# A new order of VectorE, ScalarE and TensorE instructions from the last attention pair to the third expert, one split on GpSimd, and the last store in three pieces

## Chip, cores and metric

The kernel runs on one core of one Trainium2 chip. The metric is the device time of one execution in microseconds (us); lower is better. PE is TensorE, DVE is VectorE, ACT is ScalarE, POOL is GpSimd, and SP is the queue that issues the loads and stores.

## What is computed

One layer on 256 tokens of width 512, in float32, of three parts. The first is cross attention of the tokens to 4096 context rows and to themselves. The second is causal self attention with 16 heads and compressed queries and keys. The third, the one that fills the second half of the time, is a mixture of experts:

```python
scores = sigmoid(x @ router_w)                       # 32 experts in 8 groups
...                                                  # best 4 groups, best 8 experts in them
routed = sum over the chosen e of weight_e * (silu(x @ w_gate[e]) * (x @ w_up[e])) @ w_down[e]
shared = silu(x @ sw_gate) * (x @ sw_up) @ sw_down
return routed + shared
```

Each part works on a layer-normed input and adds its result to the residual.

## The kernel before

All 32 experts are computed for all 256 tokens and weighted, with weight 0 for those not chosen. The shared expert is cut in two and stands in front, so there are `NE` = 34 experts, numbered from 0.

**Split products.** Each float32 matrix product is made of three products of rounded parts (`product`, L410, L413, L414): a_hi b_hi, a_lo b_hi and a_hi b_lo. For every weight tile that comes from memory, ACT therefore rounds `raw` to `w_hi` (`split_hi`, L278) and DVE computes `w_lo` = `raw` - `w_hi` (`split_lo`, L283). For a result that goes into a later product, ACT reads the bank to the high part (L306 and L326, `out_hi`, `half_hi`) and DVE the low part (L310 and L331, `out_lo`, `half_lo`). The values of attention, the normed tokens and the hidden rows of each expert all pass this way: PE to ACT to DVE to PE.

**Tiles.** Weight tiles are numbered through the whole program and lie in two slots in turn. An expert's tile (896 + 640 KB) has three parts: k = 0 (128x1280: gate, and the first quarter of up), k = 1 (128x1024: down) and k = 2 (128x768: the rest of up). SP loads part 0 with one transfer, and parts 1 and 2 with another (part b). Each transfer waits until the low part of the tile that had the slot has been made (`load`, L362). All loads stand in one queue.

**Order.** There is no scheduler. Each engine has one list of instructions, written out by hand or in a loop, and runs it strictly in order; engines wait for one another on counting semaphores. An instruction that waits therefore holds all that stand behind it on its engine.

**The stretch around the change** (229 to 282 us of the trace):
- The last attention pair, for the first half h = 0 and the second half h = 1 of the tokens. PE makes scores (`score_last`), DVE masks them and takes the row maximum (`last_bias`, L1331, L1396), ACT takes exponentials (`last_exps`, L1053), DVE divides by their sum (`last_normalize`, L1402, L1407), PE transposes (`transpose_last`, L773), ACT and DVE split (`last_probs_hi`, `last_probs_lo`), PE multiplies with the values (`values_last`), ACT and DVE split again, and PE makes the output product (`out_pair`) with part 1 of the attention tile. The output product of the pair before, tile 27, is mixed in.
- The third layer norm (`add_to_residual` L1143, `norm_stats` L1128 to L1132, the root on POOL L1566, `normalize` L1138) and transposes of the tokens.
- Experts 0 and 1 in another form (`expert_rows`): the hidden rows come out by token, are multiplied (`rows_hidden`, L1441) and transposed (`transpose_hidden`, L826).
- The router: PE's scores (L882), ACT's sigmoid (L1089), and on DVE a chain of some 30 small dependent instructions (L1489 to L1531) that ends in `weights`.
- From expert 2 on a loop. PE does `gate_up(j, s)` for one expert (48 products of 256 columns) and then `down` of the expert before (12 products of 512). ACT does, for each expert (`expert_step`, L1094): the silu (L1097); the splits of the next tile's part 1 and of the tile after's part 0; the rounding of the hidden rows (L1103), which waits for DVE's product; and one more split. The first of these splits waits on `used[1]`, which PE's first product of the next `gate_up` raises. DVE does `expert_hidden` (the product L1538, which ACT waits for, and the low part L1541, which waits for ACT and is what PE's `down` waits for), three splits, and `expert_add` (L1479), which adds the weighted result of both halves to the residual.
- At the end `down(0, NE - 1)`, two adds of 128x512, and two stores of 256 KB, one for each half.

## Time and profile before

| | |
|---|---|
| median of 3 runs | 546.76 us (547.22, 543.39, 546.76) |
| the profiled execution | 544.17 us |
| its span | 542.4 us |
| PE busy | 526.8 us, 97% of the span |
| DVE busy | 395.8 us, 73% |
| ACT busy | 306.5 us, 57% |
| POOL busy | 27.8 us, 5% |
| PE clock granted | 0.997 of full speed |

The page gives busy shares over the whole span. Since PE is busy nearly always, what can change lies in the few places in which it stands idle, and those are read from the timeline. Matmuls are pipelined: a product of 512 columns is followed by the next 0.23 us after its start and one of 256 columns 0.12 us after, though each is listed with a longer busy time.

### The profile page before, as it was taken

The numbers are of one execution on the slowest core, as the hardware profiler recorded it, in microseconds if no ns is written. First come the engines' busy times: TensorE is split into PE (matmuls) and PEld (weight loads), VectorE is DVE, ScalarE is ACT, GpSimd is POOL, SyncE is SP. The second block draws the span as 40 slices with busy tenths as digits, with TensorE's granted clock in tenths as the row PEclk, the third lists the DMA queues.
The fourth block names the chain that finished last, engine by engine and source line by source line (L and its number), as shares of the span: only waits on it lengthen the run. The fifth ranks groups of instructions, "written<-read, shape, count | busy, mean of one in ns | idle before, by whom it ended". The sixth has DMA issues, their size and how long they took to land.

```text
span 542.4 us, 9701 instructions
## 1 busy us (share of the span) xinstructions
PE 526.8 (97%) x3450; PEld 479.8 (88%) x3450; DVE 395.8 (73%) x646; ACT 306.5 (57%) x477; POOL 27.8 (5%) x42
## 2 busy tenths in 40 slices
PE   9999999999979999979999999999999999999997
PEld 7888888887879999959889999999999999999996
DVE  6776666558887888885887777686776867767674
ACT  4754597654456676664654645546464464645631
POOL 1000000000142223100000000000000000000000
PEclk9999999999999999999999999999999999999999
DMA  8776524455013322544435564655646455464521
GB/s 286 257 229 194 195 80 156 157 173 187 15 39 113 112 77 89 168 143 158 147 136 199 175 204 153 223 169 179 198 157 224 160 188 196 158 223 157 193 69 39
DMA packets 19283, 86.50 MB, mean 159 GB/s; under 512 B 2144, under 2 KB 2144, under 8 KB 19168
## 3 DMA queue, kind: packets, MB, share of 16 engines
q1 hardware_dynamic: 19264, 86.25, 47.4%
q8 instruction: 11, 0.18, 0.1%
q14 instruction: 8, 0.07, 0.0%
HBM read 85.72 MB, written 0.52 MB: 159 GB/s over the span
## 4 chain that ended last, share of the span: by engine, by line
PE 87%; DVE 8%; DMA 2%; ACT 1%; issue 1%; POOL 0%; DVEq 0%; SPq 0%
PE bank L410 29%; PE bank L413 28%; PE bank L414 28%; DVE w_lo L283 2%; DMA raw<-ctx_t_dram 1%; PE bank L548 1%; DVE operands L310 1%; PE bank L696 1%; DMA first_rows<-x_dram 1%; DVE first_rows L1479 1%; DVE w_lo L300 0%; DVE xt_lo L331 0%; DVE stat L1128 0%; DVE first_rows L1143 0%; PE bank L430 0%
## 5 line engine op out<-in xcount | busy, mean ns | idle before, releaser
L278 ACT CAST w_hi<-raw 128x768 fp32r<-128x768 f32 (+1 forms) x158 | 160.2, 1044 | 128.4 <-PE bank L410 120.4
L283 DVE TENSOR_TENSOR w_lo<-raw,w_hi 128x768 fp32r<-128x768 f32 (+1 forms) x158 | 187.6, 1229 | 6.7 <-ACT w_hi L278 4.7
L410 PE MATMUL bank<-xt_hi,w_hi 128*128 128x256 f32 x544 | 154.0, 283 | 0.1
L414 PE MATMUL bank<-xt_hi,w_lo 128*128 128x256 f32 x544 | 153.9, 283 | 0.0
L413 PE MATMUL bank<-xt_lo,w_hi 128*128 128x256 f32 x544 | 153.9, 283 | 0.0
L410 PE MATMUL bank<-w_hi,operands 128*128 128x512 f32 (+1 forms) x320 | 125.5, 392 | 3.1 <-DVE operands L331 1.4
L413 PE MATMUL bank<-w_lo,operands 128*128 128x512 f32 (+1 forms) x320 | 123.3, 385 | 0.0
L414 PE MATMUL bank<-w_hi,operands 128*128 128x512 f32 (+1 forms) x320 | 123.1, 385 | 0.0
L410 PEld LDWEIGHTS bank<-xt_hi,w_hi 128*128 128x128 f32 x544 | 104.3, 192 | 1.8 <-issue 0.5
L413 PEld LDWEIGHTS bank<-xt_lo,w_hi 128*128 128x128 f32 x544 | 104.3, 192 | 1.2
L414 PEld LDWEIGHTS bank<-xt_hi,w_lo 128*128 128x128 f32 x544 | 104.3, 192 | 0.0
L410 PEld LDWEIGHTS bank<-w_hi,operands 128*128 128x128 f32 x320 | 60.3, 188 | 14.6 <-DVE operands L331 1.8
L1479 DVE SCALAR_TENSOR_TENSOR first_rows<-bank,weights,first_rows 128x512 f32<-128x512 f32 x68 | 50.7, 750 | 28.7 <-PE bank L414 28.7
L414 PEld LDWEIGHTS bank<-w_hi,operands 128*128 128x128 f32 x320 | 60.1, 188 | 12.5
L413 PEld LDWEIGHTS bank<-w_lo,operands 128*128 128x128 f32 x320 | 60.4, 189 | 9.8
L310 DVE TENSOR_TENSOR operands<-bank,operands 128x512 fp32r<-128x512 f32 (+2 forms) x81 | 47.9, 625 | 22.1 <-ACT operands L306 21.9
L306 ACT ACTIVATE operands<-bank 128x512 fp32r<-128x512 f32 (+2 forms) x81 | 40.1, 549 | 35.5 <-PE bank L414 15.9
L1541 DVE TENSOR_TENSOR operands<-scores,operands 128x512 fp32r<-128x512 f32 x32 | 22.1, 692 | 40.8 <-ACT operands L1103 40.8
L410 PE MATMUL bank<-operands 128*128 128x256 f32 (+2 forms) x110 | 31.6, 287 | 3.9 <-DVE operands L310 3.9
L413 PE MATMUL bank<-operands 128*128 128x256 f32 (+2 forms) x110 | 31.9, 290 | 0.0
L414 PE MATMUL bank<-operands 128*128 128x256 f32 (+2 forms) x110 | 31.7, 289 | 0.0
L410 PEld LDWEIGHTS bank<-operands 128*128 128x128 f32 x110 | 21.6, 197 | 5.0 <-DVE operands L310 3.3
(154 smaller groups left out, 524.3 us busy)
## 6 DMA issues: line engine op xcount, KB each, us to landing
raw<-w_exp_dram SPq DMA_DIRECT2D x34, 896.0 KB, 4.7
raw<-w_exp_dram SPq DMA_DIRECT2D x34, 640.0 KB, 5.6
raw<-ctx_t_dram SPq DMA_DIRECT2D x16, 512.0 KB, 4.9
raw<-ctx_n_dram SPq DMA_DIRECT2D x16, 512.0 KB, 4.3
raw<-w_mla_dram SPq DMA_DIRECT2D x16, 512.0 KB, 4.3
raw<-wq_dram SPq DMA_DIRECT2D x4, 256.0 KB, 5.0
raw<-wk_dram SPq DMA_DIRECT2D x2, 512.0 KB, 7.1
raw<-wv_dram SPq DMA_DIRECT2D x2, 512.0 KB, 4.1
```

Source lines behind the costliest of these rows:

```text
L278: act.copy(w_hi[:, t.slot, at:at + n], raw[:, t.slot, at:at + n]).then_inc(hi_split[k], 1)
L283: eng.tensor_tensor(w_lo[:, t.slot, at:at + n], raw[:, t.slot, at:at + n], w_hi[:, t.slot, at:at + n].bitcast(F32), ALU.subtract) \
L306: act.activation(hi, bank[b][rows, at:at + n], ACT.Copy, scale=scale).then_inc(ev_hi, 1)
L310: dve.tensor_tensor(lo, bank[b][rows, at:at + n], hi.bitcast(F32), ALU.subtract) \
L410: ins = pe.matmul(o, a[0], b[0], start=start, stop=False)
L413: pe.matmul(o, a[0], b[1], start=False, stop=False)
L414: return pe.matmul(o, a[1], b[0], start=False, stop=stop)
L548: ins = pe.transpose(bank[2 * ring + h][:, k * P:k * P + P], probs[:, ring, h, k * P:k * P + P], ident)
L696: ins = pe.transpose(bank[2 + hd][:, dst:dst + P], pair_probs[:, hd, src:src + P], ident)
L1479: dve.scalar_tensor_tensor(out=res[:, h, :], in0=bank[b][:, :], scalar=w, in1=res[:, h, :], op0=ALU.mult, op1=ALU.add).then_inc(res_done, 1)
L1541: dve.tensor_tensor(h_lo[:, s % 2, :], h_row[:, s % 2, :], h_hi[:, s % 2, :].bitcast(F32), ALU.subtract).then_inc(ev_lo, 1)
```

## The change

The work is the same but for the pieces of the last expert. Its parts:
- (a) DVE no longer makes the low part of part 1 of the last attention tile (a 128x1024 `split_lo` between `last_bias(1)` and `last_normalize(0)`). POOL does, after its last turn of queries.
- (b) On DVE `last_probs_lo(0)` stands before `last_normalize(1)`, and `half_lo(4)` before the split of part 2 of expert 0. On ACT the exponentials of h = 1 are taken apart, with the split of part 2 of expert 0 and `last_probs_hi(0)` between them.
- (c) On PE the second head's output product of tile 27 for h = 1 comes after `values_last(0)`.
- (d) On DVE the split of part 0 of expert 1 (128x1280) moves from before `add_to_residual(1)` to behind `norm_stats(1)`. On PE the transposes of the second half's tokens move into the middle of `expert_rows(1, 0)`.
- (e) On DVE the split of part 0 of expert 2 (128x1280) moves from behind `rows_hidden(1, 1)` to before it.
- (f) On DVE the hidden product and the low part of expert 2 move from behind the router's chain into it.
- (g) The last `down` is made in three pieces (h = 0 with 512 columns, h = 1 with twice 256, the last of them in bank 0), each with its add and its store.

```diff
-            for h in range(2):
-                sp.wait_ge(res_done, 4 + 2 * NE - 1 + h)
-                sp.dma_start(out[:, h, :], res[:, h, :]).then_inc(stored, 16)
-            sp.wait_ge(stored, 32)
+            for k, (h, at, n) in enumerate(((0, 0, 512), (1, 0, 256), (1, 256, 256))):
+                sp.wait_ge(res_done, 4 + 2 * NE - 1 + k)
+                sp.dma_start(out[:, h, at:at + n], res[:, h, at:at + n]).then_inc(stored, 16)
+            sp.wait_ge(stored, 48)
...
-            def out_pair(t, first=False, last=False, halves=(0, 1)):
...
-                    for hd in range(2):
+                    for hd in heads:
                         ins = product(bank[h][:, :], (mo_hi[:, hd, half(h)], mo_lo[:, hd, half(h)]),
                                       wcols(t, OFF[1] + hd * 512, 512), first and hd == 0, last and hd == 1)
                     if last:
                         ins.then_inc(bank_full[h], 1)
-                if not last and 1 in halves:
+                if not last and 1 in halves and 1 in heads:
                     ins.then_inc(used[1], 1)
...
             out_pair(Tile(0, T_M + PAIRS - 2), halves=(0,))
             transpose_last(0)
-            out_pair(Tile(0, T_M + PAIRS - 2), halves=(1,))
+            out_pair(Tile(0, T_M + PAIRS - 2), halves=(1,), heads=(0,))
             pe.wait_ge(ev_lo, n)
             values_last(0)
+            out_pair(Tile(0, T_M + PAIRS - 2), halves=(1,), heads=(1,))
             transpose_last(1)
             pe.wait_ge(ev_lo, n + 1)
...
-            def expert_rows(s, h, b, told=None, split=None):
+            def expert_rows(s, h, b, told=None, split=None, midway=None):
                 t = Tile(0, T_E + s)
                 for u in range(2):
+                    if u == 1 and midway is not None:
+                        midway()
...
             expert_rows(0, 0, 4, split=V_LN3)
-            transpose_half(xn, 1, 0, xn_ready, 6)
-            expert_rows(1, 0, 5)
+            expert_rows(1, 0, 5, midway=lambda: transpose_half(xn, 1, 0, xn_ready, 6))
             expert_rows(0, 1, 6, split=V_LN3 + 2)
             expert_rows(1, 1, 7, told=used[2])
...
-            down(0, NE - 1)
+            def down_last():
+                s = NE - 1
+                t = Tile(0, T_E + s)
+                pe.wait_ge(ev_lo, V_H + s)
+                ready(t, 1)
+                for h, b, at, n in ((0, 6, 0, 512), (1, 7, 0, 256), (1, 0, 256, 256)):
+                    if b > 5:
+                        pe.wait_ge(res_done, 2 * s + h + 1)
+                    for m in range(2):
+                        a = slice(m * T + h * P, m * T + h * P + P)
+                        ins = product(bank[b][:, 0:n], (h_hi[:, s % 2, a], h_lo[:, s % 2, a]),
+                                      wcols(t, OFF[1] + m * 512 + at, n), m == 0, m == 1)
+                    ins.then_inc(bank_full[b], 1)
+            down_last()
...
-            def last_exps(h):
...
-            last_exps(0)
-            last_exps(1)
+            for hd in range(2):
+                last_exp(0, hd)
+            split_hi(act, Tile(0, T_E), 2, E_SIZES, first=True)
+            last_exp(1, 0)
             last_probs_hi(0)
-            split_hi(act, Tile(0, T_E), 2, E_SIZES, first=True)
+            last_exp(1, 1)
             half_hi(act, 4, F4["o_last"], mo_hi, 0, 2)
             last_probs_hi(1)
             split_hi(act, Tile(0, T_E + 1), 0, E_SIZES)
@@ -1414,24 +1433,24 @@
...
             last_bias(0)
             pair_out_lo(n - 1)
             last_bias(1)
-            split_lo(dve, Tile(0, T_M + PAIRS - 1), 1, M_SIZES)
             last_normalize(0)
+            last_probs_lo(0)
             last_normalize(1)
-            last_probs_lo(0)
+            half_lo(dve, 4, n + 1, mo_hi, mo_lo, 0, 2)
             split_lo(dve, Tile(0, T_E), 2, E_SIZES)
-            half_lo(dve, 4, n + 1, mo_hi, mo_lo, 0, 2)
             last_probs_lo(1)
             add_to_residual(0, F01["y"], 0, 3)
             norm_stats(0)
             half_lo(dve, 5, n + 3, mo_hi, mo_lo, 1, 2)
             normalize(0, 7)
-            split_lo(dve, Tile(0, T_E + 1), 0, E_SIZES)
             add_to_residual(0, F01["y"], 1, 4)
             tokens_lo(dve, 2, V_LN3, xt_hi, xt_lo, 0)
             norm_stats(1)
+            split_lo(dve, Tile(0, T_E + 1), 0, E_SIZES)
             normalize(1, 8)
             split_lo(dve, Tile(0, T_E + 1), 2, E_SIZES)
             tokens_lo(dve, 0, V_LN3 + 2, xt_hi, xt_lo, 1)
+            dve.wait_ge(lo_split[1], Tile(0, T_M + PAIRS - 1).split(1))
             split_lo(dve, Tile(0, T_E), 1, E_SIZES)
...
             split_lo(dve, Tile(0, T_E + 1), 1, E_SIZES)
             rows_hidden(0, 1)
+            split_lo(dve, Tile(0, T_E + 2), 0, E_SIZES)
             rows_hidden(1, 1)
-            split_lo(dve, Tile(0, T_E + 2), 0, E_SIZES)
             out_lo(dve, 0, V_H, h_hi[:, 0, :], h_lo[:, 0, :], 512)
             split_lo(dve, Tile(0, T_E + 2), 2, E_SIZES)
             out_lo(dve, 1, V_H + 1, h_hi[:, 1, :], h_lo[:, 1, :], 512)
...
+            def expert_product(j, s):
+                dve.wait_ge(silu_ready, j * 2 + (s - 1))
+                up = 2 * (s % 2) + 1
+                dve.wait_ge(bank_full[up], j + ((F01 if s % 2 == 0 else F23)["moe"] + s // 2))
+                dve.tensor_tensor(h_row[:, s % 2, :], bank[up][:, :], gate_act[:, s % 2, :], ALU.mult) \
+                   .then_inc(h_ready, 1)
+            def expert_lo(j, s):
+                dve.wait_ge(ev_hi, j * 2 + (V_H + s))
+                dve.tensor_tensor(h_lo[:, s % 2, :], h_row[:, s % 2, :], h_hi[:, s % 2, :].bitcast(F32),
+                                  ALU.subtract).then_inc(ev_lo, 1)
+            def expert_hidden(j, s):
+                expert_product(j, s)
+                expert_lo(j, s)
...
             then(dve.tensor_tensor(g_two[:, 32:48], g_top[:, 0:16], g_two[:, 16:32], ALU.add))
+            expert_product(1, 0)
...
             then(dve.tensor_tensor(beats, beats, ties, ALU.add))
+            expert_lo(1, 0)
             then(dve.tensor_reduce(rank, beats.rearrange("p (g k) -> p g k", k=GROUPS), AX, ALU.add))
...
-            def expert_hidden(j, s):
...
+            def expert_splits(j, s):
+                split_lo(dve, Tile(j, T_E + s + 1), 1, E_SIZES)
+                for k in (0, 2):
+                    split_lo(dve, Tile(j, T_E + s + 2), k, E_SIZES)
+            def last_add():
+                s = NE - 1
+                for h, b, full, at, n in ((0, 6, F6["moe"] + s // 2, 0, 512), (1, 7, F7["moe"] + s // 2, 0, 256),
+                                          (1, 0, F01["moe"] + NE // 2, 256, 256)):
+                    dve.wait_ge(bank_full[b], full)
+                    dve.wait_ge(res_done, 3 + 2 * s + h)
+                    dve.scalar_tensor_tensor(out=res[:, h, at:at + n], in0=bank[b][:, 0:n], scalar=weights[:, h, s:s + 1],
+                                             in1=res[:, h, at:at + n], op0=ALU.mult, op1=ALU.add).then_inc(res_done, 1)
             expert_add(0, 1)
-            with dve.Fori(1, NE // 2 - 1) as j:
+            expert_splits(1, 0)
+            expert_add(1, 0)
+            expert_hidden(1, 1)
+            expert_splits(1, 1)
+            expert_add(1, 1)
+            with dve.Fori(2, NE // 2 - 1) as j:
...
+                    expert_splits(j, s)
                     expert_add(j, s)
             expert_add(0, NE - 2)
-            expert_add(0, NE - 1)
+            last_add()
...
+            pool.wait_ge(lo_split[1], Tile(0, T_M + PAIRS - 1).split(1) - 1)
+            split_lo(pool, Tile(0, T_M + PAIRS - 1), 1, M_SIZES)
```

Below, the order on DVE at the three places of which the prediction speaks. DVE from the last `m_bias` (L1396; L1415 after) on, before: `w_lo` is a split, `m_inv` and the L1407 rows are `last_normalize`.

```order
L1396 TENSOR_SCALAR m_bias<-m_max,q_neg 128x2
L283 TENSOR_TENSOR w_lo<-raw,w_hi 128x1024
L1402 RECIPROCAL m_inv<-m_sum 128x2
L1407 TENSOR_SCALAR scores<-scores,m_inv 128x128 x2
L1402 RECIPROCAL m_inv<-m_sum 128x2
L1407 TENSOR_SCALAR scores<-scores,m_inv 128x256 x2
L310 TENSOR_TENSOR operands<-bank,operands 128x256
L283 TENSOR_TENSOR w_lo<-raw,w_hi 128x768
L331 TENSOR_TENSOR operands<-bank,operands 128x2x128
L310 TENSOR_TENSOR operands<-bank,operands 128x512
```

And after (L1421 and L1426 are `last_normalize`, L310 is `last_probs_lo(0)`, L331 is `half_lo(4)`):

```order
L1415 TENSOR_SCALAR m_bias<-m_max,q_neg 128x2
L1421 RECIPROCAL m_inv<-m_sum 128x2
L1426 TENSOR_SCALAR scores<-scores,m_inv 128x128 x2
L310 TENSOR_TENSOR operands<-bank,operands 128x256
L1421 RECIPROCAL m_inv<-m_sum 128x2
L1426 TENSOR_SCALAR scores<-scores,m_inv 128x256 x2
L331 TENSOR_TENSOR operands<-bank,operands 128x2x128
L283 TENSOR_TENSOR w_lo<-raw,w_hi 128x768
L310 TENSOR_TENSOR operands<-bank,operands 128x512
```

The 128x1024 split is gone, and the low part of the h = 0 probabilities and `half_lo(4)` have moved up. DVE around the second row of `rows_hidden` (L1441; L1460 after) for the second half, before (the 128x1280 split is expert 2's part 0, the L310 row behind it the low part of expert 0's hidden rows):

```order
L283 TENSOR_TENSOR w_lo<-raw,w_hi 128x1024
L1441 TENSOR_TENSOR scores<-bank,scores 128x256 x2
L283 TENSOR_TENSOR w_lo<-raw,w_hi 128x1280
L310 TENSOR_TENSOR operands<-bank,operands 128x512
L283 TENSOR_TENSOR w_lo<-raw,w_hi 128x768
```

And after:

```order
L283 TENSOR_TENSOR w_lo<-raw,w_hi 128x1024
L1460 TENSOR_TENSOR scores<-bank,scores 128x256
L283 TENSOR_TENSOR w_lo<-raw,w_hi 128x1280
L1460 TENSOR_TENSOR scores<-bank,scores 128x256
L310 TENSOR_TENSOR operands<-bank,operands 128x512
L283 TENSOR_TENSOR w_lo<-raw,w_hi 128x768
```

The split stands one row earlier. DVE in the router's chain, from L1500 (L1535 after) on, before:

```order
L1500 TENSOR_TENSOR scores<-scores 128x16
L1510 TENSOR_TENSOR scores<-scores 128x128
L1511 TENSOR_TENSOR scores<-scores 128x128
L1512 TENSOR_TENSOR scores<-scores,smalls 128x128
L1513 TENSOR_TENSOR scores<-scores 128x128
L1514 TENSOR_REDUCE scores<-scores 128x16
L1515 TENSOR_SCALAR scores<-scores 128x16
```

And after (L1505 is the hidden product of expert 2, L1510 its low part, L1549 and L1551 are rows of the router's chain):

```order
L1535 TENSOR_TENSOR scores<-scores 128x16
L1505 TENSOR_TENSOR scores<-bank,scores 128x512
L1546 TENSOR_TENSOR scores<-scores 128x128
L1547 TENSOR_TENSOR scores<-scores 128x128
L1548 TENSOR_TENSOR scores<-scores,smalls 128x128
L1549 TENSOR_TENSOR scores<-scores 128x128
L1510 TENSOR_TENSOR operands<-scores,operands 128x512
L1551 TENSOR_REDUCE scores<-scores 128x16
L1552 TENSOR_SCALAR scores<-scores 128x16
L1554 TENSOR_TENSOR scores<-scores 128x64
```

The product and the low part now stand within the chain; everything from L1551 to the `weights`, and `expert_add(0, 1)` behind them, comes after the low part.

## Rows read from the trace of the kernel before

**Rows 1.** The page, part 1: busy time, share of the span, instructions
```profile
PE 526.8 (97%) x3450; PEld 479.8 (88%) x3450; DVE 395.8 (73%) x646; ACT 306.5 (57%) x477; POOL 27.8 (5%) x42
```

**Rows 2.** Timeline of PE, 231 to 282 us (start us, busy us, instruction, [idle before <-releaser])
```profile
234.12 0.44 PE L773 MATMUL bank<-first_rows,scores 128*128 128x128 f32 x2 [1.22 <-DVE scores L1407]
...
237.51 0.50 PE L410 MATMUL bank<-w_hi,operands 128*128 128x512 f32 x1 [0.48 <-DVE operands L331]
...
241.41 0.50 PE L410 MATMUL bank<-w_hi,operands 128*128 128x512 f32 x1 [0.96 <-DVE operands L331]
...
244.85 0.35 PE L410 MATMUL bank<-w_hi,xt_hi 128*128 128x256 f32 x1 [1.35 <-DVE xt_lo L331]
...
259.95 0.50 PE L410 MATMUL bank<-w_hi,operands 128*128 128x512 f32 x1 [0.67 <-DVE operands L310]
...
278.38 0.49 PE L410 MATMUL bank<-w_hi,operands 128*128 128x512 f32 x1 [0.71 <-DVE operands L1541]
...
281.24 0.28 PE L410 MATMUL bank<-xt_hi,w_hi 128*128 128x256 f32 x1
```

**Rows 3.** Timeline of DVE, 232 to 244 us
```profile
232.26 1.22 DVE L283 TENSOR_TENSOR w_lo<-raw,w_hi 128x1024 fp32r<-128x1024 f32 x1
...
233.39 0.16 DVE L1402 RECIPROCAL m_inv<-m_sum 128x2 f32<-128x2 f32 x1
...
242.16 1.48 DVE L283 TENSOR_TENSOR w_lo<-raw,w_hi 128x1280 fp32r<-128x1280 f32 x1
...
243.56 0.68 DVE L1143 TENSOR_TENSOR first_rows<-bank,first_rows 128x512 f32<-128x512 f32 x1
```

**Rows 4.** Timelines of ACT and DVE, 228 to 238 us
```profile
228.99 1.04 ACT L278 CAST w_hi<-raw 128x1024 fp32r<-128x1024 f32 x1
...
234.60 0.38 ACT L306 ACTIVATE operands<-bank 128x256 fp32r<-128x256 f32 x1 [0.93 <-PE bank L773]
...
235.01 0.42 DVE L310 TENSOR_TENSOR operands<-bank,operands 128x256 fp32r<-128x256 f32 x1 [0.22 <-ACT operands L306]
...
237.03 0.42 DVE L331 TENSOR_TENSOR operands<-bank,operands 128x256 fp32r<-128x256 f32 x1 [0.33 <-ACT operands L326]
```

**Rows 5.** Timelines of POOL and DVE, 161 to 176 us
```profile
161.67 0.73 POOL L353 TENSOR_TENSOR scores<-scores 128x256 f32<-128x256 f32 x1
...
174.23 1.60 POOL L353 TENSOR_TENSOR scores<-scores 128x256 f32<-128x256 f32 x1
...
173.76 1.47 DVE L283 TENSOR_TENSOR w_lo<-raw,w_hi 128x1024 fp32r<-128x1024 f32 x1
```

**Rows 6.** Line L368, 233 to 234 us: the load of the second expert's parts b
```profile
DMA to landing us min/median/max: 4.7/4.7/4.7
```

**Rows 7.** Timeline of DVE, 257 to 285 us
```profile
257.82 1.48 DVE L283 TENSOR_TENSOR w_lo<-raw,w_hi 128x1280 fp32r<-128x1280 f32 x1
...
263.26 0.22 DVE L1483 COPY scores<-bank 128x64 f32<-128x64 f32 x1 [1.90 <-PE bank L882]
...
271.18 0.29 DVE L1514 TENSOR_REDUCE scores<-scores 128x16 f32<-128x128 f32 x1
...
274.77 1.41 DVE L1479 SCALAR_TENSOR_TENSOR first_rows<-bank,weights,first_rows 128x512 f32<-128x512 f32 x2
...
278.07 3.49 DVE L283 TENSOR_TENSOR w_lo<-raw,w_hi 128x1024 fp32r<-128x1024 f32 x3
...
284.37 0.69 DVE L1541 TENSOR_TENSOR operands<-scores,operands 128x512 fp32r<-128x512 f32 x1 [0.90 <-ACT operands L1103]
```

**Rows 8.** Timeline of ACT, 272 to 284 us
```profile
272.07 2.21 ACT L278 CAST w_hi<-raw 128x1024 fp32r<-128x1024 f32 x2 [5.14 <-PE bank L410]
...
283.73 0.61 ACT L1103 CAST operands<-scores 128x512 fp32r<-128x512 f32 x1
```

**Rows 9.** The end: timeline of DVE, and line L398 (the stores)
```profile
539.16 0.75 DVE L1479 SCALAR_TENSOR_TENSOR first_rows<-bank,weights,first_rows 128x512 f32<-128x512 f32 x1 [0.61 <-PE bank L414]
...
DMA to landing us min/median/max: 2.0/2.0/2.0
```

22 lines of the change are left out of this document (6 added, 16 removed).

## Prediction

> **What bounds the kernel now.** I read the busy shares first: PE is busy 526.8 of 542.4 us, DVE only 395.8 [rows 1]. PE's work is not changed but for a few pieces at the end, so the change can only move the 15.6 us in which PE stands idle. Next I listed PE's waits from 228 us on, with the timeline. There are six, and they are the rows that carry a bracket [rows 2]: 1.22, 0.48, 0.96, 1.35, 0.67 and 0.71 us. After 278.38 PE never waits again until the last store. The rest of the idle time lies ahead of 228 us, where no instruction moves. The brackets count from the modelled end of the product before. Counted from when PE would have issued the next instruction, the gaps are about 0.15 longer: 1.37, 0.65, 1.13, 1.51, 0.82 and 0.88, in all 6.4 us. That and the tail behind the last product is all that can be won: about 1.2% of the time.
>
> **The change, gap by gap** (times as in the trace of before; what is won shifts all that follows).
>
> Gap 1, before the transposes of h = 0. They wait for `last_normalize(0)`. On DVE the 1024-column split starts at 232.26 and the reciprocal at 233.39 [rows 3], so the split that moves to POOL takes 1.13 out of this chain. The exponentials it needs are ready before. Left: 1.37 - 1.13 = 0.24.
>
> Gap 2, before the last output product. The transposes now start at 232.99. From them to the low part done is 234.12 to 234.60 to 235.01 plus 0.42, so 1.31 us [rows 2, 4], and 0.05 to PE: `values_last(0)` can start at 234.35. PE has two transposes and only three products (0.20 + 0.78) before it and is free at 233.97: a new gap of 0.38. From the last of these products over ACT and `half_lo(4)` to PE is 1.2 us (0.42 of it the DVE row at 237.03 [rows 4]). Before, four transposes (0.45) covered part of it. Now three products of 0.23 and the transposes cover 1.15: no gap. For h = 1 `last_probs_lo(1)` comes out some 0.10 late. So gaps 1 and 2, 2.02 before, become 0.72.
>
> Gap 3: values, ACT, `half_lo(5)`, output product. The chain is the same, with nothing put between: 1.13 becomes about 1.08, since `var_eps` no longer stands right ahead.
>
> Gap 4, before the first expert product. The split of expert 1's part 0 holds DVE from 242.16, and `add_to_residual(1)` starts behind it at 243.56 [rows 3]. PE had finished bank 1 at 243.1, so moving the split wins 0.46: 1.51 becomes 1.05. Where the split goes, behind `norm_stats(1)`, it needs 1.4 us, and `expert_rows(1, 0)` is due about 1.8 us after it starts there. The second layer norm then waits for it, but its transposes now have a half `expert_rows` more. I cost that at nothing; without this cover it would be at most the 1.4 of the split.
>
> Gap 5, before the first `down`. The chain is PE, silu, `rows_hidden(1, 1)`, the 1280-column split (from 257.82, 1.40 to the next start [rows 7]), the low part. With the split one place earlier, where DVE is idle, the low part is ready some 0.3 before PE wants it: 0.82 becomes 0.
>
> Sum so far: before 1.37 + 0.65 + 1.13 + 1.51 + 0.82 = 5.48; after 0.24 + 0.38 + 0.10 + 1.08 + 1.05 = 2.85. PE is **2.63 us ahead** at the first `down`.
>
> The split on POOL: its nearest row is a subtraction-like instruction of 256 columns, 0.73 us alone and 1.60 beside a DVE split [rows 5]. For 1024 columns that is 2.9 alone (four times 0.73) and 6.4 if it were always shared. It starts at 230.1, when ACT's high part is there (from 228.99, 1.04 [rows 4]). From then until about 236 DVE's instructions read at most one operand of SBUF, and DVE's list has no split there. So I take 2.9: done at 233.0, against 233.5 on DVE before. Its users are the last output product (due 236.1) and the transfer of expert 1's part b, which lands 4.7 us after it is issued [rows 6], at 237.8; ACT wants it at 238.0. Both fit, barely. DVE's added wait for this split comes at 249 and costs nothing.
>
> The Trainium skill speaks against this part: "GPSIMD Engine Reference", section Key points, says that VectorE is structurally about twice as fast for elementwise work, and that GpSimd shares its SBUF interfaces with VectorE instructions that have two SBUF inputs. The pair 0.73 and 1.60 of this trace shows the second, and the DVE split beside it took 1.47 rather than 1.22. From its 4497 ns for 2048 columns (section Performance versus the Vector engine) an estimate for 1024 is 2.3 us. By that the sum stays what it is.
>
> **Gap 6, where most of it is lost again.** In before DVE works almost without idle from 263.26 to 281.5 [rows 7]: copy of the scores, three splits, two adds, router chain, two adds, `expert_hidden`, splits. PE waits 0.88 for the hidden rows at 278.38 and then starts the `gate_up` of expert 4 at 281.24; its part 0 was ready at 278.07 + 1.13 + 1.48 = 280.68. Now the low part of expert 2 stands inside the router's chain, and waits for ACT's rounding. ACT's rounding stands behind two splits, and the first waits for PE's first product of expert 3's `gate_up`: it came at 272.07 [rows 8], now at 269.44. In the next round the rounding begins 2.12 after the first of the two splits (the two show 2.21 busy) and the low part 284.37 - 283.73 = 0.64 after it [rows 7, 8]. So `expert_lo(1, 0)` cannot start before 269.44 + 2.12 + 0.64 = 272.20. DVE reaches it earlier: the copy is at 260.63, ACT's high part lets the splits start at 261.0, then 3.40 of splits, 1.32 of adds, 1.76 of small instructions, 0.62 for the product and 1.30 for four more: 269.4. **DVE stands for 2.8 us**, with the rest of the chain queued behind it. After it come 0.61 for the low part itself, 3.59 for the rest of the chain (271.18 to 274.77), 1.32 for `expert_add(0, 1)`, 1.13 for one split, and 1.48 for expert 4's part 0: 280.33, and PE starts at 280.38. PE is ready for it at 277.6. So the gap of 0.88 goes and one of 2.8 comes, at another tile. Against 281.24 PE has won 0.86, less 0.07 for a first product after a stop: **0.79**. From there the loop has slack, 8.5 us of PE against 5.9 of DVE for an expert, and no gap follows.
>
> Put generally: from PE's first product of expert 3 to that of expert 4 it is now 11.35 us by the DVE chain, against 9.50 before. What the first five gaps give (2.63) is cut by about 1.84.
>
> **The tail.** PE's last half now has 12 products of 256 columns, one each 0.12, rather than six of 512, one each 0.23: 0.07 more. The last add has 256 columns instead of 512, some 0.48 instead of 0.75 [rows 9]: 0.27 less. The last store is 128 KB instead of 256 KB. It took 2.0 us to land [rows 9]; between nothing and the 0.4 that half the bytes need I take 0.25. Sum 0.45.
>
> [...]
>
> **Sum:** 0.79 + 0.45 = 1.24 us. The profiled execution took 544.17 us (its span 542.4 and 1.8 around it): 542.9. But the median of the three runs is 546.76, and the four executions known lie in two pairs, 543.4 and 544.2, 546.8 and 547.2. A median may fall in either. I state the forecast against the mean of the four, 545.4: 544.1.
>
> **Rivals.**
> - *DVE does not stand in the router's chain.* The last gap closes too, and the saving is 2.63 + 0.88 + 0.45 = 4.0 us: 541.4. For it: the chain's work alone (16.5 us from 261.0) ends at 277.5, just when PE wants expert 4. Against it: ACT's row at 272.07, whose wait is on PE, and the order of ACT is not changed there. Chance 0.15.
> - *The early waits only move.* Each of gaps 1 to 5 is a round of PE, ACT, DVE and PE of about 1.2 us with little work to cover it. If the new places are some tenths tighter than I have them (0.3 at gap 5, 0.2 at expert 1's part b), the lead is 1.84 or less, nothing is left after gap 6, and only the tail is won: 545.0. Chance 0.2.
> - *The split on POOL is slow, and the kernel slower.* At the shared rate of 6.4 us it ends at 236.5. Expert 1's part b is then issued at 236.6 and lands at 241.3. ACT's split of part 2 (0.83) waits for it, and `half_hi(5)` stands behind on ACT: 242.1 instead of 239.2. That costs 2.9, the lead is -0.3, and with the 1.84 less the tail the change costs 1.7: 547.1. It decides from an end of the POOL split at 233.55 on, since ACT has 0.33 to spare: 0.5 us from what I forecast. For it: POOL's seven 256-column additions took 1.60 in six cases. Against it: there DVE had a split, here it has none. Chance 0.1.
> - My forecast has 0.55.
>
> **Range and chances.** The rivals reach from 541.4 to 547.1; the two pairs of before put 1.3 to 1.8 us on either side of the centre. 540.8 to 546.8 leaves out about 2 in 10. For the likeliest case alone it is 542.2 to 546.0. A change of 1% (5.4 us) is about what a measurement can tell from none; even all gaps closed would barely reach it. Faster 0.04, same 0.94, slower 0.02.
>
> **What would show it.** Right: a single wait of DVE of nearly 3 us for ACT's rounding before L1510 inside the router's chain; a wait of PE of about 2.7 us for `w_lo` before the first product of expert 4; no wait of PE before the first `down`; four small ones of 0.1 to 1.1 between 232 and 243; a POOL split of 2 to 3 us from 230.1. Wrong: a POOL split over 3.5 us with ACT waiting for a transfer near 238; PE waiting for something else between 243 and 269; or no wait of PE after 269, which would be the first rival.

## Result: slower by half a per cent, where a gain of 1.2 us was forecast

The changed kernel took **547.63 us** in the median of 20 runs (545.15 to 551.14). The kernel before, measured beside it, took 545.08 (20 runs, 543.39 to 547.36). The ratio is 1.0049, with a 95% interval of 1.0033 to 1.0065: 2.6 us slower. It lies within the 1% named ahead, but the sign is the other one, and 547.6 is above the range. The profiled execution took 548.39 us (span 546.6), 4.2 us more than that of before.

One measure is used throughout. Nothing differs between the kernels ahead of `last_bias(0)`, but executions vary there. So I count **from the start of `last_bias(0)` on DVE** (0.54 ahead of the first `m_bias<-m_max,q_neg` row) **to the end of the span**: 229.84 to 542.4 before, 312.56 us; 229.46 to 546.6 after, 317.14. That is 4.58 us longer.

### The profile after

Page of the changed kernel, parts 1 and 2: what answers to [rows 1], and the TensorE clock in 40 slices.

```profile
PE 529.9 (97%) x3456; PEld 481.8 (88%) x3456; DVE 397.1 (73%) x646; ACT 306.4 (56%) x477; POOL 31.4 (6%) x43
PEclk9999999999999999979989999999999999999999
```

PE is *busy* 3.1 us longer than before with all but the same work (six small products more at the end). The clock line says where to look: a 7 where the change begins (232 to 246 us) and an 8 at expert 4 (273 to 287). It has to be read first, before any wait.

Timeline of PE in the changed kernel, the waits behind 228 us (columns as in [rows 2]):

```profile
232.82 0.69 PE L410 MATMUL bank<-w_hi,operands 128*128 128x512 f32 x1 [1.94 <-DVE operands L310]
...
242.97 0.62 PE L410 MATMUL bank<-w_hi,operands 128*128 128x512 f32 x1 [0.93 <-DVE operands L331]
...
247.24 0.36 PE L410 MATMUL bank<-w_hi,xt_hi 128*128 128x256 f32 x1 [0.67 <-DVE xt_lo L331]
...
284.54 0.58 PE L410 MATMUL bank<-xt_hi,w_hi 128*128 128x256 f32 x1 [2.67 <-DVE w_lo L283]
```

Four waits, 6.21 us, against six with 5.39 before [rows 2]. The first is new, and the last is the forecast one.

Timelines of DVE and POOL in the changed kernel, at the new POOL split and at the root behind it:

```profile
230.00 2.18 DVE L1415 TENSOR_SCALAR m_bias<-m_max,q_neg 128x2 f32<-128x2 f32 x1
232.09 0.68 DVE L310 TENSOR_TENSOR operands<-bank,operands 128x512 fp32r<-128x512 f32 x1
...
233.48 0.23 DVE L1415 TENSOR_SCALAR m_bias<-m_max,q_neg 128x2 f32<-128x2 f32 x1
...
248.38 1.48 DVE L283 TENSOR_TENSOR w_lo<-raw,w_hi 128x1280 fp32r<-128x1280 f32 x1
...
229.79 2.36 POOL L283 TENSOR_TENSOR w_lo<-raw,w_hi 128x1024 fp32r<-128x1024 f32 x1 [11.73 <-ACT w_hi L278]
...
248.54 1.74 POOL L1611 TENSOR_TENSOR rstd<-var_eps,power 128x1 f32<-128x1 f32 x1 [5.57 <-DVE var_eps L1151]
```

Two numbers per partition take 2.18 us instead of the 0.23 of the same instruction at 233.48. It is busy, not idle, so no bracket shows it; what shows it is its end: 232.18, and POOL's split ends at 232.15. DVE stood still for 1.95 us inside an instruction. `pair_out_lo(n - 1)` stands right behind (232.09), and PE waits for that at 232.82.

Windows of the changed kernel, cut at the changes of the clock (columns: window, PE, PEld, DVE, ACT, POOL busy, granted clock, DMA share, GB/s):

```profile
228.00:232.50 4.50, 2.88 (x25) 2.68 (x24) 3.73 (x8) 1.83 (x3) 2.36 (x1) 1.00 0.62 257
232.50:236.50 4.00, 3.68 (x10) 2.90 (x11) 1.73 (x9) 2.48 (x9) 0.00 (x0) 0.57 0.82 267
236.50:243.00 6.50, 5.51 (x34) 4.16 (x33) 5.34 (x12) 4.35 (x8) 0.56 (x1) 1.00 0.20 81
243.00:247.00 4.00, 3.58 (x10) 2.51 (x10) 1.57 (x3) 1.16 (x3) 0.00 (x0) 0.57 0.00 0
247.00:284.00 37.00, 34.62 (x254) 32.42 (x254) 27.98 (x61) 17.83 (x24) 1.74 (x1) 1.00 0.35 128
284.00:288.00 4.00, 3.46 (x18) 3.46 (x18) 3.30 (x6) 2.73 (x3) 0.00 (x0) 0.57 0.83 263
```

Three stretches at 0.57 (mostly 1.2 GHz, the lower of the two levels; 1.00 is 2.4). Each begins in the last moments of a wait of PE or right behind it: 1.94, 0.93 and 2.67 us. The page "TensorE: Matmul & The Clock Gate" of the Trainium skill, section "HAM oscillation — how this bites in real kernels", says that stalls between bursts of products bring the clock down, and that each costs a stretch at half rate. The trace agrees in kind, with these three rows. It differs in size: the stalls of the page's example are some 3 to 5 us long, and here the clock fell behind 0.93 to 2.67.

What a stretch costs is seen in the runs: 20 of the changed kernel, by granted clock of the whole execution, were 546.0 us at 0.997 (5 runs), 547.3 at 0.994 (4), 548.6 at 0.991 (7) and 550.5 at 0.988 (4). (550.5 - 546.0) / 3 = **1.5 us for each 0.003**, which is one stretch. The profiled execution, at 0.991, has three. The kernel before shows the same steps, in its runs beside the experiments (96 runs; two slow ones, of 551.0 and 743.3 us, are left out): 543.8 us at 0.999 or 1.000 (33 runs), 545.5 at 0.996 or 0.997 (43) and 547.1 at 0.993 or 0.994 (13). So at the same clock the two kernels are only 0.2 to 0.5 us apart; what differs is how often the clock falls. None of the 20 runs of the changed kernel had a clock above 0.997.

Timelines of DVE and ACT in the changed kernel, at expert 2's rounding, against [rows 7, 8]:

```profile
276.35 0.69 DVE L1510 TENSOR_TENSOR operands<-scores,operands 128x512 fp32r<-128x512 f32 x1 [2.81 <-ACT operands L1122]
...
273.52 2.21 ACT L278 CAST w_hi<-raw 128x1024 fp32r<-128x1024 f32 x2 [4.78 <-PE bank L410]
275.63 0.61 ACT L1122 CAST operands<-scores 128x512 fp32r<-128x512 f32 x1
```

The wait in the router's chain is the forecast one: 2.81 us, behind two splits and a rounding on ACT.

The end of the changed kernel, against [rows 9]: DVE, and landing of the three stores.

```profile
542.52 1.20 DVE L1583 SCALAR_TENSOR_TENSOR first_rows<-bank,weights,first_rows 128x512 f32<-128x512 f32 x2 [0.61 <-PE bank L414]
543.95 0.48 DVE L1583 SCALAR_TENSOR_TENSOR first_rows<-bank,weights,first_rows 128x256 f32<-128x256 f32 x1 [0.23 <-PE bank L414]
...
DMA to landing us min/median/max: 1.7/2.0/2.1
```

### The profile page after: what moved, and what is told of

It is laid out like the page before. It is cut to its first block, busy times and chain, and to the rows that moved or that the text cites. A ratio compares the mean times of both kernels' runs of the same rounds, so it can differ in the third digit from the quotient of the medians.

```text
span 546.6 us, 9702 instructions
## 1 busy us (share of the span) xinstructions
PE 529.9 (97%) x3456; PEld 481.8 (88%) x3456; DVE 397.1 (73%) x646; ACT 306.4 (56%) x477; POOL 31.4 (6%) x43
## 4 chain that ended last, share of the span: by engine, by line
PE 89%; DVE 6%; DMA 2%; ACT 1%; issue 1%; POOL 0%; DVEq 0%; ACTq 0%; SPq 0%
PE bank L410 29%; PE bank L414 29%; PE bank L413 29%; DMA raw<-ctx_t_dram 2%; PE bank L548 1%; DVE w_lo L283 1%; DVE operands L310 1%; PE bank L696 1%; DMA first_rows<-x_dram 1%; DVE w_lo L300 0%; ACT w_hi L278 0%; PE bank L430 0%; DVE xt_lo L331 0%; DVE m_bias L1415 0%; DVE rope_w L1194 0%
## 5 line engine op out<-in xcount | busy, mean ns | idle before, releaser
L283 DVE TENSOR_TENSOR w_lo<-raw,w_hi 128x1024 fp32r<-128x1024 f32 (+2 forms) x157 | 186.3, 1228 | 8.8 <-ACT w_hi L278 6.8
L410 PE MATMUL bank<-w_hi,operands 128*128 128x512 f32 (+1 forms) x322 | 127.0, 394 | 3.8 <-DVE operands L310 1.9
L413 PE MATMUL bank<-w_lo,operands 128*128 128x512 f32 (+1 forms) x322 | 124.7, 387 | 0.0
L414 PE MATMUL bank<-w_hi,operands 128*128 128x512 f32 (+1 forms) x322 | 124.4, 386 | 0.0
L410 PEld LDWEIGHTS bank<-w_hi,operands 128*128 128x128 f32 x322 | 61.1, 190 | 15.2 <-DVE operands L310 2.1
L414 PEld LDWEIGHTS bank<-w_hi,operands 128*128 128x128 f32 x322 | 61.1, 190 | 12.6
L1498 DVE SCALAR_TENSOR_TENSOR first_rows<-bank,weights,first_rows 128x512 f32<-128x512 f32 x66 | 49.2, 750 | 28.5 <-PE bank L414 28.4
L310 DVE TENSOR_TENSOR operands<-bank,operands 128x512 fp32r<-128x512 f32 (+2 forms) x81 | 47.9, 625 | 24.2 <-ACT operands L306 23.9
L1510 DVE TENSOR_TENSOR operands<-scores,operands 128x512 fp32r<-128x512 f32 x32 | 22.2, 693 | 42.9 <-ACT operands L1122 42.9
L410 PE MATMUL bank<-operands 128*128 128x256 f32 (+2 forms) x110 | 31.1, 283 | 3.9 <-DVE operands L310 3.9
L413 PE MATMUL bank<-operands 128*128 128x256 f32 (+2 forms) x110 | 31.1, 282 | 0.0
L414 PE MATMUL bank<-operands 128*128 128x256 f32 (+2 forms) x110 | 31.0, 282 | 0.0
```

Source lines behind the costliest of these rows:

```text
L283: eng.tensor_tensor(w_lo[:, t.slot, at:at + n], raw[:, t.slot, at:at + n], w_hi[:, t.slot, at:at + n].bitcast(F32), ALU.subtract) \
L310: dve.tensor_tensor(lo, bank[b][rows, at:at + n], hi.bitcast(F32), ALU.subtract) \
L410: ins = pe.matmul(o, a[0], b[0], start=start, stop=False)
L413: pe.matmul(o, a[0], b[1], start=False, stop=False)
L414: return pe.matmul(o, a[1], b[0], start=False, stop=stop)
L1498: dve.scalar_tensor_tensor(out=res[:, h, :], in0=bank[b][:, :], scalar=w, in1=res[:, h, :], op0=ALU.mult, op1=ALU.add).then_inc(res_done, 1)
```

## The experiments

Theory: the loss has three parts. DVE is held by the POOL split, the low part of expert 2 stands too early in the router's chain, and PE's clock falls behind both waits. Rivals: any DVE instruction is held by POOL, whatever its form; the clock falls by chance, whatever PE did; the first gaps and the tail don't give what was forecast. Each ratio below is to the kernel before, measured beside the run, with its 95% interval in brackets. The times from `last_bias(0)` on and the waits are those of one profiled execution each.

**Undoing and doing one part alone.** `undo_pool` puts the split back on DVE:

```diff
             last_bias(1)
+            split_lo(dve, Tile(0, T_M + PAIRS - 1), 1, M_SIZES)
             last_normalize(0)
...
-            dve.wait_ge(lo_split[1], Tile(0, T_M + PAIRS - 1).split(1))
...
-            pool.wait_ge(lo_split[1], Tile(0, T_M + PAIRS - 1).split(1) - 1)
-            split_lo(pool, Tile(0, T_M + PAIRS - 1), 1, M_SIZES)
```

> The changed kernel with the low part of the last attention tile's part 1 back on DVE, ahead of last_normalize(0). Theory P (a DVE instruction of the 2.18 us m_bias kind waits for the whole of POOL's 2.36 us split, and the PE gap of 2 us that follows brings PE down to half clock): the 128x2 m_bias takes 0.23 us again, PE's gap of 1.9 us at the last output product of tile 27 goes, no half-clock stretch follows there, and about 3.5 us come back: 2.4 us less than the changed kernel at least, within 1 us of before. DVE's wait for the rounding of expert 2 stays near 2.8 us, and PE's before expert 4. Rival Q (all of the loss comes from that late wait and its half clock; the POOL stall is absorbed, since DVE stands in the router's chain anyway): the time stays 2 to 3 us over before.

Measured: ratio 1.0012 (0.9985 to 1.004), 315.26 us from `last_bias(0)`. PE's waits are 1.21, 0.23, 0.93, 0.90 and 2.66 us. The 1.94 is gone, the 1.21 of before is back, and no stretch at half clock is left between 230 and 250. But the wait at expert 4 stands, with two stretches' worth of half clock behind it. So the hold is undone as the theory says, and the time is still 2.70 us over before, as the rival had it, not within 1 us.

`undo_f` puts `expert_hidden(1, 0)` back behind `expert_add(0, 1)`:

```diff
-            expert_product(1, 0)
...
-            expert_lo(1, 0)
...
             expert_add(0, 1)
+            expert_hidden(1, 0)
             expert_splits(1, 0)
```

> The changed kernel with the hidden product and low part of expert 2 behind the router's chain and the adds again. POOL keeps its split. Theory P: the early loss stays (m_bias 2.2 us, half clock after it), the late gap of 2.7 us and its half clock go and a gap of 0.7 to 0.9 at expert 2's down comes back; 1 to 2.5 us over before. Rival Q: faster than before by 1 us or more, since the late wait was all.

Measured: 1.0011 (0.9979 to 1.0042), 313.99 us. The 2.67 is gone and a wait of 1.05 for the hidden rows is back. 1.93, 0.93 and 0.67 stand as in the changed kernel, with two stretches at half clock. That is 1.43 us over before, within the 1 to 2.5 expected.

`undo_pool_f` is both together.

> Both undone. Theory P: PE is 1.5 to 2.6 us ahead at the first down, one gap of 0.9 stays at expert 2's down, the last store gives 0.5: 2 to 3 us faster than before. Rival Q: 1 to 2 us faster. A third theory R (the clock's low stretches come by chance and not by gaps): the low stretches stay, and the time is within 1 us of before.

Measured: 0.9978 (0.9952 to 1.0005), **311.02 us**, 1.54 less than before. The clock is 1.00 all through the changed stretch. The gain is that of the rival (1 to 2 us), not the theory's 2 to 3, but it is one: the rest of the change wins, and these two parts lose it.

`pool_only` is the kernel before with the same four lines about the split moved to POOL.

> The kernel before with nothing changed but the split of the last attention tile's part 1 on POOL. Theory P: m_bias takes 2.2 us as in the changed kernel, the output product of tile 27 waits about 1.9 us, 1.13 us come back before last_normalize(0), and the clock falls after the gap: 1.5 to 3 us slower than before. Rival Q: within 1 us of before.

Measured: 1.0015 (0.9985 to 1.0045), 314.58 us, 2.02 more. Its timelines of DVE and POOL:

```profile
231.06 2.17 DVE L1396 TENSOR_SCALAR m_bias<-m_max,q_neg 128x2 f32<-128x2 f32 x1
...
230.84 2.36 POOL L283 TENSOR_TENSOR w_lo<-raw,w_hi 128x1024 fp32r<-128x1024 f32 x1 [11.73 <-ACT w_hi L278]
```

The hold needs nothing else of the change.

The ratios of these four all have 1 in their intervals. What they do tell apart is the changed kernel (1.0033 to 1.0065) from `undo_pool_f` (0.9952 to 1.0005): together the two parts lose the time. What each costs alone is read from the traces.

`f_only` is the kernel before with the product and the low part of expert 2 moved into the router's chain, as the change has it.

> The kernel before with the hidden product and the low part of expert 2 within the router's chain, and nothing else. By the sum of the prediction DVE waits 2.7 to 3.0 us for the rounding, expert 2's down no longer waits (0.9 back), expert 4 waits 2.8, so 1.85 us more, and a half-clock stretch of 1.4 to 3 us at double length behind it: last_bias(0) to the end 315.5 to 317.5 us against 312.6. Rival: DVE's wait is hidden where nothing else is ahead, and the time is within 0.5 us of before.

Measured: 1.0037 (1.0007 to 1.0067), 317.14 us, 4.58 more. Windows of `f_only`:

```profile
284.00:288.00 4.00, 1.33 (x6) 0.92 (x5) 4.00 (x5) 0.24 (x1) 0.00 (x0) 0.80 0.32 61
288.00:292.00 4.00, 4.00 (x21) 4.00 (x21) 3.30 (x5) 3.88 (x5) 0.00 (x0) 0.50 0.84 322
292.00:296.00 4.00, 4.00 (x29) 3.96 (x29) 2.61 (x3) 1.31 (x2) 0.00 (x0) 0.85 0.67 214
```

DVE waited 3.15 us for ACT's rounding, PE 2.67 for `w_lo`, and then PE ran at half clock for twice as long as behind the other waits. (The profiled execution of `f_only`, 552.8 us, also had a long stretch at half clock from 163 us on, ahead of all that differs.)

The half clock behind this wait is not certain. Five of the 12 runs of `f_only` had a clock of 1.000, so no such stretch anywhere. They took 545.5 us on the mean, 1.7 more than the 543.8 of the kernel before at 0.999 or 1.000 beside them (13 runs), near the +1.97 that the longer waits alone give. No trace of these five was kept.

**Which instruction does POOL hold?** `odd_bias` is the changed kernel with `m_bias` written by two instructions of one column:

```diff
-                k = slice(2 * h, 2 * h + 2)
-                dve.tensor_scalar(m_bias[:, k], m_max[:, k], q_neg[:, h:h + 1], None, ALU.mult) \
-                   .then_inc(m_bias_ready, 1)
+                for k in (2 * h, 2 * h + 1):
+                    ins = dve.tensor_scalar(m_bias[:, k:k + 1], m_max[:, k:k + 1], q_neg[:, h:h + 1], None, ALU.mult)
+                ins.then_inc(m_bias_ready, 1)
```

> The changed kernel with the last pair's m_bias, a 128x2 product, made as two of 128x1. Theory P1 (what waits for POOL's split is a DVE instruction in a fast mode that one tensor in SBUF, one result in SBUF and an even count bring about, as the 128x2 has): the two 128x1 take about 0.2 us each though POOL's split of 2.4 us runs beside them, PE's gap of 1.9 us goes, and with it the half-clock stretch after it. From last_bias(0) to the end 312.7 to 314.3 us against 312.6 of before and 317.1 of the changed kernel. Rival P2 (any DVE instruction whose scalar comes from a pointer, or that reads only SBUF, waits for POOL): one of them still takes about 2.1 us and the time stays.

Measured: 1.0001 (0.9973 to 1.0029), 313.14 us, 4.0 less than the changed kernel. Timelines of `odd_bias`, DVE, POOL and PE:

```profile
230.40 0.34 DVE L1415 TENSOR_SCALAR m_bias<-m_max,q_neg 128x1 f32<-128x1 f32 x2
...
230.20 2.40 POOL L283 TENSOR_TENSOR w_lo<-raw,w_hi 128x1024 fp32r<-128x1024 f32 x1 [11.73 <-ACT w_hi L278]
...
234.49 0.33 PE L410 MATMUL bank<-operands 128*128 128x128 f32 x1 [0.23 <-DVE operands L310]
...
280.75 0.38 PE L410 MATMUL bank<-xt_hi,w_hi 128*128 128x256 f32 x1 [2.67 <-DVE w_lo L283]
```

Both `m_bias` instructions run inside POOL's split in 0.34 us, and so do `pair_out_lo` and the maximum rows of h = 1 behind them. The rival (any DVE instruction is held) falls. What is held is the form 128x2, SBUF to SBUF. The Trainium skill, "Advanced Engine Details and Errata", section Mode Summary, names such a form: a fast mode through two read ports, with source and destination in SBUF and their sizes both even, or both odd, above one and equal; its note says that GPSIMD and these instructions block each other, since the second port is shared. The two pairs of rows (two columns held, one column not) fit that rule, though no row names the mode, and an odd size above one was not tried.

**Does the low part only stand too early?** `odd_late` is `odd_bias` with `expert_lo(1, 0)` later in the chain:

```diff
             then(dve.tensor_tensor(beats, beats, ties, ALU.add))
-            expert_lo(1, 0)
...
                 then(dve.match_replace(replaced[:, h * E:h * E + E], top8[:, h * TOP:h * TOP + TOP], m, TAKEN))
+            expert_lo(1, 0)
             then(dve.tensor_tensor(picked, replaced, masked, ALU.not_equal))
```

> As odd_bias, and the low part of expert 2 stands 13 instructions later in the router's chain, ahead of the comparison that follows the second match. If DVE's wait there is what costs PE 2.7 us and the half clock behind it, DVE waits under 0.5 us, PE does not wait before expert 4, and last_bias(0) to the end is 308.5 to 309.5 us: 3 to 4 us faster than before (ratio 0.993 to 0.995). Rival: PE waits for expert 4's part 0 anyway, since DVE's work of 16.5 us alone fills the time; then 1 us or more is missing.

Measured: 0.9963 (0.9932 to 0.9993), 309.55 us. Timelines of `odd_late`, DVE and PE:

```profile
272.25 0.69 DVE L1510 TENSOR_TENSOR operands<-scores,operands 128x512 fp32r<-128x512 f32 x1 [0.74 <-ACT operands L1122]
...
278.38 0.39 PE L410 MATMUL bank<-xt_hi,w_hi 128*128 128x256 f32 x1 [0.61 <-DVE w_lo L283]
```

2.07 us of small instructions of the router run before ACT is done, instead of behind it. So DVE waits 0.74 instead of 2.81, PE 0.61 instead of 2.67, and the clock stays at 1.00. Less than 0.5 and nothing were expected for these two; where the 0.61 comes from, `best` below shows.

`mid_late` has that too, but the split of part b on DVE, between `last_normalize(0)` and `last_probs_lo(0)`, and nothing on POOL.

> No split on POOL: DVE makes it between last_normalize(0) and last_probs_lo(0), where it idled 1 us; the low part of expert 2 late as in odd_late. If POOL is of no use here, this is as fast as odd_late within 0.7 us: last_bias(0) to the end 309 to 310 us. If the load behind this split (issued some 1 us later) holds ACT up before half_hi(5), PE's gap there grows by 0.3 to 1 us.

Measured: 0.9967 (0.9941 to 0.9993), 309.82 us. Waits of 0.33, 1.23, 0.89 and 0.61, against 0.23, 0.93, 0.90 and 0.61 for `odd_late`. The other place on DVE is as good as POOL to 0.3 us: the split need not leave DVE.

**What brings the clock down?** `fill` is `odd_bias` with 12 products of zeros for PE in the place of the 2.67 us. They are work beside the computation; the loop's first round is written out, as it is:

```diff
+            gate_up(1, 1, told=used[1])
+            down(1, 0, told=used[2])
+            pe.wait_ge(h_ready, 1)
+            for _ in range(12):
+                zeros(0, True)
+            gate_up(1, 2, told=used[1])
+            down(1, 1, told=used[2])
-            with pe.Fori(1, NE // 2 - 1) as j:
+            with pe.Fori(2, NE // 2 - 1) as j:
```

> The changed kernel with m_bias as two 128x1 instructions (so odd_bias), and 12 extra products of zeros on TensorE, once VectorE's product for expert 2 is there and before expert 4's first product, where odd_bias showed TensorE waiting 2.67 us and then half the clock for some 7 us. The zeros are work beside the computation. If the empty stretch ahead is what brings the clock down (theory): the trace shows 1.00 behind that place, TensorE waits there for at most about 1 us in one piece, and from the start of last_bias(0) to the end it takes 311.5 us (odd_bias: 313.1), with an end of the router chain that stays where it was. Rival, the clock falls there by itself or by the heavier load after it, whatever TensorE did before: the half clock stays and it takes 313 us or more.

Measured: **0.9972** (0.9951 to 0.9994), where `odd_bias` had 1.0001: the intervals overlap, but doing more was not slower. Timeline of PE in `fill`:

```profile
278.61 2.88 PE L476 MATMUL bank<-zero_r 128*128 128x512 f32 x12
281.44 0.39 PE L410 MATMUL bank<-xt_hi,w_hi 128*128 128x256 f32 x1
```

Windows of `fill`:

```profile
240.00:244.00 4.00, 3.46 (x10) 2.38 (x9) 1.53 (x4) 1.00 (x3) 0.00 (x0) 0.57 0.00 0
...
281.00:285.00 4.00, 4.00 (x33) 3.63 (x31) 3.31 (x6) 3.00 (x4) 0.00 (x0) 1.00 0.91 281
```

The same window of `odd_bias`:

```profile
281.00:285.00 4.00, 4.00 (x23) 4.00 (x23) 3.31 (x6) 3.58 (x4) 0.00 (x0) 0.57 0.79 304
```

At 281 us PE does 33 products in 4 us, where it did 23. With the empty stretch filled, the clock does not fall: there the theory holds. But the time from `last_bias(0)` was 312.89 us, not 311.5. This execution has a stretch at half clock at 240 to 244, behind waits of 0.23 and 0.93, which `odd_bias` has at the same places without one. So a short wait may or may not be followed by the lower clock, and half of the rival stands for short waits. Over the runs the mean granted clock was 0.9952 in `odd_bias` and 0.9970 in `fill`; 4 of 12 runs of `fill` had 0.999 or 1.000, none of `odd_bias`.

**What is left.** `best` is `odd_late` with two lines exchanged:

```diff
-            expert_add(0, 1)
             expert_splits(1, 0)
+            expert_add(0, 1)
             expert_add(1, 0)
```

> odd_late with the three splits for experts 3 and 4 ahead of the sum of expert 1 in VectorE's list. In odd_late the sum stood ahead of the splits and TensorE waited 0.61 us ahead of expert 4 with its clock at 1.00. Theory (that gap is the time of what stands ahead of the splits in VectorE's list): the gap goes, 308.9 us from the start of last_bias(0) to the end against 309.55, ratio to the kernel before about 0.995. Rival (the late sum holds banks 6 and 7, and TensorE waits for them at expert 2's down product instead): a wait of 0.5 us or more at a bank of the sums appears, and the time stays at 309.5 or rises.

Measured: **0.9941** (0.9919 to 0.9963), 542.15 us in the median, 308.65 us from `last_bias(0)`. No wait of PE is left behind 250 us, and none for banks 6 and 7. This version beats both kernels, by 0.6% and, from the two ratios, by 1.1%.

`tail_only` is the kernel before with the three-piece end alone:

```diff
-            for h in range(2):
+            for k, (h, at, n) in enumerate(((0, 0, 512), (1, 0, 256), (1, 256, 256))):
...
-            down(0, NE - 1)
+            down_last()
...
-            expert_add(0, NE - 1)
+            last_add()
```

> The kernel before with the last down product, last sum and last store in three pieces and nothing else of the change. Theory (the tail's gain is its own and stands apart from the rest): from the first product of the last expert's second half to the end 4.3 us where the kernel before has 4.8, last_bias(0) to the end 312.05 us against 312.56, ratio 0.999. Rival (what the tail wins is lost elsewhere, or exists only with the rest of the change): 312.5 us, ratio 1.000.

Measured: 312.07 us, 0.49 less than before, as expected. The ratio, 1.0001 (0.9976 to 1.0027), can't tell half a microsecond from none.

**The balance.** For each profiled execution: the difference of PE's waits behind 228 us to the 5.39 of before, -0.52 where the end is in three pieces, and 1.5 for each stretch at half clock behind 228 us (a stretch of double length counts as two); then what was measured from `last_bias(0)` on.

| kernel | waits of PE | end | half clock | sum | measured |
|---|---|---|---|---|---|
| changed | +0.82 | -0.52 | 3 x 1.5 | +4.80 | +4.58 |
| `undo_pool` | +0.54 | -0.52 | 2 x 1.5 | +3.02 | +2.70 |
| `undo_f` | -0.81 | -0.52 | 2 x 1.5 | +1.67 | +1.43 |
| `undo_pool_f` | -1.05 | -0.52 | 0 | -1.57 | -1.54 |
| `pool_only` | +0.69 | 0 | 1 x 1.5 | +2.19 | +2.02 |
| `f_only` | +1.97 | 0 | 2 x 1.5 | +4.97 | +4.58 |
| `odd_bias` | -0.66 | -0.52 | 1 x 1.5 | +0.32 | +0.58 |
| `fill` (waits with the 2.83 of zeros) | -0.73 | -0.52 | 1 x 1.5 | +0.25 | +0.33 |
| `mid_late` | -2.33 | -0.52 | 0 | -2.85 | -2.74 |
| `odd_late` | -2.72 | -0.52 | 0 | -3.24 | -3.01 |
| `best` | -3.33 | -0.52 | 0 | -3.85 | -3.91 |

No row misses by more than 0.4 us; each is one execution. Without the column of the clock the changed kernel would stand at +0.30.

## Why the prediction was wrong, and where it was right

**Right: the rounds of PE, ACT and DVE.** Gaps in the prediction's own count are 0.15 longer than the brackets. `odd_bias`, where POOL holds nothing, shows 0.23, 0.93, 0.90 and 2.67 in brackets, so 0.38, 1.08, 1.05 and 2.82. Forecast were 0.38, 1.08, 1.05 and 2.8. Gap 5 is gone, as said. The two small rests (0.24 ahead of the transposes, 0.10 at h = 1) show no bracket. So "PE is 2.63 us ahead" and "gap 6, where most of it is lost again" both hold. Without the half clock `odd_bias` would stand at 0.58 - 1.5 = -0.9, against the -1.24 forecast.

**Right: the tail.** From the first product of the last expert's second half to the end it was 4.80 (537.60 to 542.4) and is 4.28 (542.32 to 546.6): 0.52, forecast 0.45. The last add took 0.48 as said. The stores landed in 1.7 to 2.1 us where they took 2.0. `tail_only`, where nothing else is changed, won 0.49.

**Wrong, first step: "Both fit, barely", the split on POOL at no cost.** I sized the split (2.9 us, it was 2.36) and its users, but not what POOL does to DVE meanwhile. The condition that I set, that DVE has no instruction with two SBUF inputs there, was met, and it was not enough: a TENSOR_SCALAR with one input of two columns was held for 1.95 us. The Trainium skill, "GPSIMD Engine Reference", section Key points, names both kinds, those with two SBUF inputs and those in a two-port mode; I took over only one half of the sentence. And [rows 5] had already shown how such a pair runs: DVE's split ends at 173.76 + 1.47 = 175.23, POOL's 1.60 began at 174.23 and ended 0.60 after that. POOL stood until DVE was done and then needed 0.60, not far from its own 0.73. That is one after the other, not "a shared rate". DVE's 1.47 instead of 1.22 fits too: POOL's instructions before ran until 174.15 (173.26, 0.89 for two), 0.39 into it. In the changed kernel it shows again at 248.54: POOL's root takes 1.74, and in the kernel before 0.55 or 0.56 where DVE has no split. The third rival had the sign (the split on POOL makes the kernel slower) but not the place: no transfer came late.

**Wrong, second step: a gap of PE was priced at its own length.** The sum has no term for the clock. Over the runs the mean granted clock fell from 0.9967 (the 96 runs of before beside these experiments) to 0.9925, by 0.0042, and that is 0.0042 / 0.003 x 1.5 = 2.1 us. With +0.82 for the waits and -0.52 for the end it makes +2.4, against the 2.55 between the medians. So **the clock is the larger part of the loss**, and the forecast's wait of 2.8 us at expert 4, rightly sized, was priced at two thirds of what it cost where a stretch at half clock followed (2.8 of 2.8 + 1.5). The trace of before had the row that says so, and I did not ask for it, since the change starts behind it. Windows of the kernel before, around a wait of PE of 2.41 us that ends at 161.38:

```profile
160.00:161.00 1.00, 0.00 (x0) 0.00 (x0) 1.00 (x2) 0.70 (x2) 1.00 (x1) 1.00 0.03 8
161.00:162.00 1.00, 0.61 (x3) 0.62 (x4) 1.00 (x3) 0.00 (x0) 0.92 (x3) 0.81 0.07 8
162.00:163.00 1.00, 1.00 (x7) 1.00 (x6) 1.00 (x2) 0.00 (x0) 0.40 (x1) 0.50 0.65 213
```

The "two pairs" of the four executions of before, 543.4 and 544.2 against 546.8 and 547.2, which I took as given, may be of the same kind: the runs of before lie 1.6 to 1.7 us apart from one step of the clock to the next. It isn't shown for these four, since the clock is on record for one alone (544.17 us, 0.997).

**Rivals.** "DVE does not stand in the router's chain" fell (2.81 us). It names, though, the place where most is to be had: `odd_late` and `best` take PE's wait away by moving one subtraction, and one sum behind three splits. "The early waits only move" fell with `odd_bias`.

## What to carry to other kernels

Price a wait of TensorE at its length and at what the clock may do behind it: here some 1.5 us more for each stretch at half clock that followed, which was so behind 12 of the 20 traced waits of 1.9 us or more. Before you give VectorE's work to GpSimd, go through what VectorE does in that time for instructions with two SBUF inputs, and for those with one source, SBUF to SBUF, even if they are tiny (here two columns): they and GpSimd's instruction ran one after the other, and that wait is inside a busy time, where no bracket tells it. When an instruction that waits for another engine is put into a chain, put it as late in the chain as its own users allow.

## What the runs showed of the hardware

- A TENSOR_SCALAR of 128x2, SBUF to SBUF, took 2.18 and 2.17 us beside a POOL split of 2.36, 0.23 alone; as two of 128x1 it took 0.34 beside a POOL split of 2.40.
- POOL's subtraction of 128x1024 with two SBUF inputs took 2.36 to 2.40 us, less than four times the 0.73 of 256 columns; DVE's took 1.22.
- The clock fell in the profiled execution behind every wait of 1.93 us or more in the changed stretch (7 of 7, in 6 kernels). Behind the wait of 2.41 at 161 to 163 us, which every kernel has, it fell in 5 of the 13 profiles, that of the kernel before among them and that of the changed kernel not, with the same instructions. Behind the one of 0.93 or 0.94 it fell in 3 of 8 (the changed kernel, `undo_f` and `fill`). What decides there is open: I did not find it in a row.
- Nor does it always fall behind a long wait in the executions without a trace: 5 of 12 of `f_only` had a clock of 1.000, and 5 of 20 of the changed kernel had 0.997, room for one stretch, with two waits of 1.94 and 2.67 in its order.
- Twice, in `undo_pool` and `f_only`, the half clock behind the wait at expert 4 lasted twice as long as in `odd_bias`. Why is open too.
